# A macaron block of two layers on one core: weights of the first feed-forward pair kept, loads moved to the start, table terms placed one by one

## The chip, the core and the metric

The program runs on one NeuronCore of a Trainium2 chip. Its engines run side by side and meet only at semaphores: TensorE (PE, matrix products into the eight PSUM banks; PEld are its weight loads), VectorE (DVE), ScalarE (ACT), GpSimd (POOL) and SyncE (SP), which here only issues DMAs. Each engine takes its instructions strictly in the order of its program. The metric is the device time of one execution in microseconds (us), the median of several runs; lower is better.

## What is computed

x is 1024 tokens of 256 features. Six sublayers are added to it one after another, each behind a layer norm:

```
x = x + 0.5 * L0_ffn(norm(x))     # f=0, u=0
x = x +       L0_attn(norm(x))    #      u=1
x = x + 0.5 * L0_ffn(norm(x))     # f=1, u=2
x = x + 0.5 * L1_ffn(norm(x))     # f=2, u=3
x = x +       L1_attn(norm(x))    #      u=4, a gated delta rule
x = x + 0.5 * L1_ffn(norm(x))     # f=3, u=5

L0_ffn(x): h = silu(x @ gate_w.T * gate_s) * (x @ up_w.T * up_s);  h @ down_w.T * down_s   # 704 inner features
L1_ffn(x): the same without scales, 688 inner features, each weight = lut[idx], lut of 16 values
L0_attn:   16 heads of 128 over 4 key/value heads, rotary tables, window of 64, difference of two softmaxes, then @ Wo
```

All is float32. The weights of L1_ffn aren't given as numbers but as indices into the table of 16 values; they have to be made on the chip.

## The kernel before

X (tokens in rows) stays in SBUF. Everything else shares one buffer, `arena`, whose columns are laid out anew for each stage: `Arena(arena, start).take(...)` hands out consecutive columns. Two names with the same columns mean that the second may be written only when the first isn't needed any more; the waits see to that.

A feed-forward `ffn(f, u)` works on two halves (hf) of 512 tokens. The 704 or 688 inner features are six tiles (MT), in the order of TILES, the short one first. For each tile PE makes gate and up products (`ffn_up`, lines 631 and 639) into two pairs of banks, ACT takes the SiLU of the gate (`silu`, L998), DVE multiplies with up (`ffn_hidden`, L1344 for f < 2, L1348 else): this is h, and `h_done` counts it. PE may fill a pair of banks again only when the h of the tile two before is done. The down-product (`ffn_down`, L658) of a half wants all six h of it; it is made in two pairs of token tiles, and DVE adds each to X (`ffn_add`, L1359 scales, L1362 adds, and gives `x_ready`). PE's order in a stage: six tiles of half 0; transposes of half 1 of the normed x (`ln_turn`, L614; ACT copies them to XT, L987); two tiles of half 1; down-product of half 0; four tiles of half 1; transposes of half 0 for the next stage; down-product of half 1.

The table's values. While f=0 and f=1 run, ACT and DVE make the L1 weights, half of them in each. For each of the 16 values k, ACT writes `AWAY = |FAR * idx - FAR * k|` (`away`, L1009, 128x2144), zero where idx is k and huge elsewhere; DVE folds `W1 = min(W1, AWAY - value)` (`look_up`, L1382 for k=0 and L1385, two instructions of 1072 columns). One k is called a term here. W1 then holds the negated weights, and SP stores them to DRAM (L561, L588) and loads them from there as f=2's weights. `TERMS` says how many terms stand behind each tile's h: (1, 2, 1, 2, 1, 2) in half 0 and (1, 1, 1, 2, 1, 1) in half 1. ACT has them ahead of the tile's SiLU, DVE behind the tile's h. AWAY has four slots (PENS), and ACT waits for DVE when all are in use. DVE's first sum of half 0 stands behind the second h of half 1.

SP issues the loads in one queue. `load_ffn(f)` loads WU (gate and up), WD (down) and DS (down's scale), in that order, three DMAs, 48 on `w_loaded`; PE and DVE start stage f when 48 * (f + 1) is reached. WU1, the L1 gate and up weights, has the same columns as WU. The attention lays its own tiles over all of these columns, so f=1 loads the f=0 weights again, with the indices' second half into IDX, when the attention's sums are done (`x_ready` 8); f=2's load waits for `x_ready` 12, the end of f=1. The attention's key and value weights WKV lie in OT's last columns at the top of the arena; a_wkv is issued behind `x_ready` 4 and `xt_ready` 8, with the rotary tables, masks and first WQ behind it.

In the attention PE makes keys, values and queries (`rope_project` L686, `values` L693), and then runs a staggered loop over 64 pairs of heads and token tiles (76 steps with the tail). ACT copies the weighted values into OT, 16 heads of 1024 tokens (`ot_copy`, L1063), and `weighted` (L741) multiplies them with WO a group of four heads at a time, 16 steps or more behind; DVE adds to X. The delta rule follows a hand-written table of places (PLACE), which the change doesn't touch.

## Time and profile before

| | us |
|---|---|
| median of 3 runs | 1812.22 |
| lowest, highest | 1808.32, 1816.23 |
| profiled execution | 1804.4 |
| its span, first to last instruction | 1802.4 |

The profile is of one execution. Its times count from the first instruction. A row of a timeline stands for one or more instructions of one engine and line that follow each other; the number in brackets is how long the engine stood idle before them, and the name behind the arrow is what ended the wait. Matmuls are recorded twice for each product of float32, so x8 are the four matmuls that the program has. Their ends are modelled.

The stages lie so in this execution: f=0 from 15 to 93, attention from 100 to 412, f=1 from 421 to 503, f=2 from 512 to 580, the delta rule from 584 to 1721, f=3 from 1729 to 1797.

### The profile page before, as it was taken

What the parts mean: (1) busy time and instruction counts of PE and PEld (TensorE: products, weight loads), DVE (VectorE), ACT (ScalarE), POOL (GpSimd) and SP (SyncE); (2) the same over time, 40 slices, a digit from 0 to 9 for tenths busy, and PEclk for the clock granted to TensorE, in tenths of its full rate; (3) what the DMA queues carried; (4) which work ended last, traced back from release to release, by engine and by line L of the source; (5) the groups of instructions that cost most, each with busy time, mean ns of one, the idle gap of its engine ahead of it and who ended that gap; (6) DMA issues with size and microseconds to landing.
All of it is one profiled execution on the core that took longest, in us unless ns stands there. A gap on an engine that the chain in (4) does not pass through costs nothing. (4 is left out here: it accounts for less than half of the span.)

```text
span 1802.4 us, 33031 instructions
## 1 busy us (share of the span) xinstructions
PE 1547.0 (86%) x10840; PEld 1067.9 (59%) x10840; DVE 1338.2 (74%) x3718; ACT 1034.1 (57%) x2716; POOL 41.3 (2%) x49
## 2 busy tenths in 40 slices
PE   6867889786878778999999998999999899888678
PEld 2534555563535246767766766776777677677535
DVE  6649989956722388889889889888898998984121
ACT  6317878876310455866766676586676667643210
POOL 0000000000000000000000000000000000000000
PEclk9989899989889879999999999999999999989589
DMA  2023000001010211011201101111110110100010
GB/s 103 25 75 93 11 10 5 2 1 77 25 52 18 63 29 43 16 52 51 61 12 55 58 12 57 58 38 29 57 55 12 60 54 16 45 28 7 1 52 24
DMA packets 84071, 69.42 MB, mean 39 GB/s; under 512 B 58673, under 2 KB 72625, under 8 KB 82625
## 3 DMA queue, kind: packets, MB, share of 16 engines
q1 hardware_dynamic: 83904, 67.31, 12.3%
q8 instruction: 91, 1.49, 0.3%
q14 instruction: 76, 0.61, 0.1%
HBM read 58.33 MB, written 6.98 MB: 36 GB/s over the span
## 5 line engine op out<-in xcount | busy, mean ns | idle before, releaser
L1524 DVE SCALAR_TENSOR_TENSOR arena<-arena 128x1024 f32<-128x1024 f32 x144 | 184.1, 1279 | 30.6 <-ACT arena L1101 29.8
L789 PE MATMUL bank<-xt,arena 128*128 128x512 f32 x384 | 197.4, 648 | 4.5 <-ACT arena L1093 3.1
L1582 DVE COPY_PREDICATED arena<-arena,bank 128x512 f32<-128x512 int32 x160 | 185.0, 1175 | 0.3 <-issue 0.3
L842 PE MATMUL bank<-arena 128*64 128x64 f32 x3072 | 143.8, 238 | 36.6 <-DVE arena L1604 21.7
L842 PEld LDWEIGHTS bank<-arena 128*64 128x64 f32 x3072 | 117.0, 144 | 84.0 <-issue 54.6
L1602 DVE TENSOR_TENSOR arena<-arena 128x512 f32<-128x512 f32 x224 | 156.4, 698 | 3.3 <-PE bank L842 2.9
L639 PE MATMUL bank<-xt,arena 128*128 128x512 f32 x320 | 143.5, 604 | 5.5 <-DVE arena L1344 3.9
L789 PEld LDWEIGHTS bank<-xt,arena 128*128 128x128 f32 x384 | 73.7, 209 | 74.8 <-issue 71.8
L639 PEld LDWEIGHTS bank<-xt,arena 128*128 128x128 f32 x320 | 60.3, 193 | 89.6 <-issue 83.6
L658 PE MATMUL bank<-arena 128*128 128x256 f32 (+2 forms) x384 | 102.3, 416 | 11.0 <-DVE arena L1344 10.2
L1100 ACT COPY arena<-bank 128x512 f32<-128x512 f32 x96 | 56.5, 589 | 91.7 <-PE bank L789 91.7
L1035 ACT ACTIVATE arena<-arena 128x128 f32<-128x128 f32 x256 | 99.1, 389 | 6.6 <-DVE arena L1452 6.6
L886 PE MATMUL bank<-arena 128*128 128x64 f32 x512 | 98.4, 273 | 0.0
L658 PEld LDWEIGHTS bank<-arena 128*128 128x128 f32 (+2 forms) x384 | 72.2, 200 | 42.1 <-issue 21.4
L884 PE MATMUL bank<-arena 128*128 128x64 f32 x512 | 95.5, 267 | 0.9 <-DVE arena L1624 0.5
L1211 ACT COPY arena<-bank 128x128 f32<-128x128 f32 x128 | 34.3, 268 | 104.8 <-PE bank L917 104.4
L1604 DVE TENSOR_TENSOR arena<-arena 128x256 f32<-128x256 f32 x224 | 94.1, 420 | 0.0
L686 PE MATMUL bank<-xt,arena 128*128 128x512 f32 x160 | 83.8, 652 | 10.0 <-DMA arena<-a_wkv 5.6
L1220 ACT COPY arena<-bank 128x128 f32<-128x128 f32 x128 | 34.1, 266 | 93.6 <-PE bank L925 57.4
L884 PEld LDWEIGHTS bank<-arena 128*128 128x128 f32 x512 | 79.1, 191 | 9.5 <-DVE arena L1624 6.2
L905 PEld LDWEIGHTS bank<-arena 128*128 128x128 f32 x224 | 40.5, 199 | 71.3 <-issue 42.9
L998 ACT ACTIVATE arena<-bank 128x512 f32<-128x512 f32 (+1 forms) x24 | 14.3, 596 | 117.8 <-PE bank L639 75.4
(169 smaller groups left out, 3563.6 us busy)
## 6 DMA issues: line engine op xcount, KB each, us to landing
arena<-zero_scratch SPq DMA_DIRECT2D x29, 512.0 KB, 3.8
arena<-d_w SPq DMA_DIRECT2D x16, 519.0 KB, 6.1
arena<-beta_scratch SPq DMA_DIRECT2D x16, 512.0 KB, 5.4
arena<-f_up SPq DMA_DIRECT2D x2, 1408.0 KB, 6.3
arena<-w_scratch SPq DMA_DIRECT2D x2, 1376.0 KB, 6.1
arena<-f_idx SPq DMA_DIRECT2D x2, 1072.0 KB, 9.7
w_scratch<-arena SPq DMA_DIRECT2D x2, 1072.0 KB, 4.0
arena<-a_wq SPq DMA_DIRECT2D x16, 128.0 KB, 2.7
```

The lines of the kernel that those rows point to most:

```text
L639: last = pe.matmul(bank[2 * w + n % 2][0:rows, :], (WU if f < 2 else WU1R)[:, w, k, m * P:m * P + rows], XT[:, k, hf * HALF:(hf + 1) * HAL ...
L658: last = pe.matmul(bank[4 + pair][:, j * D:(j + 1) * D], HT[0:rows, hf, m, t * P:(t + 1) * P], WD[0:rows, m, :], start=(m == 0), stop=(m = ...
L686: last = pe.matmul(bank[6 + m % 2][:], w, XT[:, k, hf * HALF:(hf + 1) * HALF], start=(k == 0), stop=(k == KC - 1))
L789: last = pe.matmul(bank[b][:], DW[:, par, c:c + P], XT[:, k, rhs], start=(k == 0), stop=(k == KC - 1))
L842: last = pe.matmul(to[:, :, p], KL[:, par, r], rhs, start=True, stop=True)
L884: pe.matmul(to[:, 0], YY[:, par, c, :], PM[:, c, :].rearrange("p (b r s) -> p b r s", r=2, s=s)[:, :, 0, :], start=True, stop=True)
L886: last = pe.matmul(to[:, 1], PM[:, c, :], YY[:, par, c, :].rearrange("p (b r s) -> p b r s", r=2, s=s)[:, :, 1, :], start=True, stop=True)
L1035: last = act.activation(EX[:, p % 2, i, a, :], SMK[:, p % 2, i, a, :], ACT.Exp, bias=NMX[:, p % 2, i, a:a + 1], scale=-1.0, accum_out=ES[: ...
L1524: dve.scalar_tensor_tensor(out=CT[:, x], in0=RAW[:, x, 3 - j:3 - j + S], scalar=DW[:, par, tap:tap + 1], in1=CT[:, x], op0=ALU.mult, op1=A ...
L1582: dve.copy_predicated(out, mask, bank[b][:].rearrange("p (c b s) -> p c b s", c=8, s=s)).then_inc(free[b], 1)
L1602: dve.tensor_tensor(kq, kq, left, ALU.mult)
L1604: dve.tensor_tensor(kl, kl, t[:, :, 1, :].broadcast_to([P, nb // 2, s]), ALU.mult).then_inc(kq_step, 1)
```

## The change

- Arena: WU, WD, DS and WKV get columns of their own at the top, beside the attention's tiles. So does IDX1, the second half of the indices. To make room OT has 8 heads' slots rather than 16, used in turn; ACT's copy into a slot waits (`wo_done`) for the product of the group two before. WU1 and WD1, the L1 weights, lie in the lower columns, apart from WU and WD.
- SP: a_wkv and the second half of f1_idx are issued at the start, behind f=0's loads. Nothing is loaded for f=1. The load for f=2 goes out when the stored weights have landed in DRAM (`w1_saved`), with no wait for `x_ready` 12. f=2 and f=3 load two tiles, without DS. The counts that PE and DVE wait for are W_COUNT = 48, 48, 80, 112.
- The terms: one behind each of the six tiles of half 0; in half 1 none behind the first h, two behind the second, then the first sum, two more, the second sum and the statistics, one behind these and one behind each of the next three h, and two behind the last. ACT's order follows it: its SiLU stands ahead of its Abs in half 1's first two tiles.

The diff, cut to its core:

```diff
-TERMS = ((1, 2, 1, 2, 1, 2), (1, 1, 1, 2, 1, 1))
+W_COUNT = 48, 48, 80, 112
+TERMS = (1, 1, 1, 1, 1, 1, 2, 2, 1, 1, 1, 1, 2)
...
-        WU = A.take(2, KC, F0)
-        WD = A.take(MT, D)
-        WU1 = arena[:, NT * D:NT * D + 2 * KC * F1]
+        WU1 = A.take(2 * KC * F1)
...
-        DS = A.take(D)
+        WD1 = A.take(MT, D)
...
-        top = arena.shape[1] - H * S
-        OT = arena[:, top:].rearrange("p (h s) -> p h s", h=H)
-        WKV = arena[:, top + (H - 2) * S:].rearrange("p (k n) -> p k n", k=KC)
+        top = arena.shape[1] - (8 * S + KC * 2 * G * P + 2 * KC * F0 + MT * D + D + LW)
+        A = Arena(arena, top)
+        OT = A.take(8, S)
+        WKV = A.take(KC, 2 * G * P)
+        WU = A.take(2, KC, F0)
+        WD = A.take(MT, D)
+        DS = A.take(D)
+        IDX1 = A.take(LW, dt=I32)
...
             def load_ffn(f):
-                up, down = (f0_up, f0_down) if f < 2 else (w1_dram[:, 0:UP1], w1_dram[:, UP1:])
-                sp.dma_start(WU1 if f >= 2 else WU, up).then_inc(w_loaded, 16)
-                sp.dma_start(WD, down).then_inc(w_loaded, 16)
+                if f:
+                    sp.dma_start(WU1, w1_dram[:, 0:UP1]).then_inc(w_loaded, 16)
+                    sp.dma_start(WD1, w1_dram[:, UP1:]).then_inc(w_loaded, 16)
+                    return
+                sp.dma_start(WU, f0_up).then_inc(w_loaded, 16)
+                sp.dma_start(WD, f0_down).then_inc(w_loaded, 16)
                 sp.dma_start(DS, f0_ds).then_inc(w_loaded, 16)
...
             sp.dma_start(IDX, f1_idx[:, 0:LW]).then_inc(idx_loaded, 16)
+            if count > 1:
+                sp.dma_start(WKV, a_wkv).then_inc(at_kv_w, 16)
+            if count > 2:
+                sp.dma_start(IDX1, f1_idx[:, LW:]).then_inc(idx_next, 16)
...
                 sp.wait_ge(xt_ready, 8)
-                sp.dma_start(WKV, a_wkv).then_inc(at_kv_w, 16)
...
                 sp.wait_ge(x_ready, 8)
-                load_ffn(1)
-                sp.dma_start(IDX, f1_idx[:, LW:]).then_inc(idx_loaded, 16)
                 sp.wait_ge(lut_acc, 4 * LUTN)
                 sp.dma_start(w1_dram[:, LW:], W1).then_inc(w1_saved, 16)
                 sp.wait_ge(w1_saved, 32)
             if count > 3:
-                sp.wait_ge(x_ready, 12)
                 load_ffn(2)
...
                 def ot_copy(p):
                     k, t = divmod(p, NT)
                     act.wait_ge(pv_done, p + 1)
-                    act.copy(OT[:, 2 * k:2 * k + 2, t * P:(t + 1) * P],
+                    wait(act, wo_done, 4 * (k // 2 - 2) + t // 2 + 1 if k > 3 else 0)
+                    act.copy(OT[:, 2 * k % 8:2 * k % 8 + 2, t * P:(t + 1) * P],
...
             def ffn(f, u):                      # ACT
+                for q in range(MT):
+                    away(f, terms(q))
+                    silu(f, 0, [q])
                 ln_copy(u, 1)
+                silu(f, 1, [0])
+                away(f, terms(MT))
+                silu(f, 1, [1])
+                away(f, terms(MT + 1))
+                for q in range(2, MT):
+                    away(f, terms(MT + q))
+                    silu(f, 1, [q])
+                away(f, terms(2 * MT))
...
```

Three places in the order of the instructions. First DVE in f=0, from the first h of half 1 (it reads small_vectors_high) to the terms behind the statistics (L1344 is an h and L1385 the terms, two rows of instructions each; L1359 and L1362 scale and add, and L1312 to L1317 are the statistics). Before:

```order
L1344 SCALAR_TENSOR_TENSOR arena<-bank,small_vectors_high,arena 64x512
L1385 SCALAR_TENSOR_TENSOR arena<-arena,small_vectors 128x1072 x2
L1344 SCALAR_TENSOR_TENSOR arena<-bank,small_vectors,arena 128x512
L1359 TENSOR_TENSOR arena<-bank,arena 128x512
L1362 SCALAR_TENSOR_TENSOR x<-arena,x 128x512
L1359 TENSOR_TENSOR arena<-bank,arena 128x512
L1362 SCALAR_TENSOR_TENSOR x<-arena,x 128x512
L1312 BN_STATS ln_stats<-x 128x6 x4
L1315 BN_AGGR ln_mean_var<-ln_stats 128x2 x4
L1317 TENSOR_SCALAR ln_var_eps<-ln_mean_var 128x4
L1385 SCALAR_TENSOR_TENSOR arena<-arena,small_vectors 128x1072 x2
```

And now (L1357 the h, L1398 the terms, L1372 and L1375 the sum):

```order
L1357 SCALAR_TENSOR_TENSOR arena<-bank,small_vectors_high,arena 64x512
L1357 SCALAR_TENSOR_TENSOR arena<-bank,small_vectors,arena 128x512
L1398 SCALAR_TENSOR_TENSOR arena<-arena,small_vectors 128x1072 x4
L1372 TENSOR_TENSOR arena<-bank,arena 128x512
L1375 SCALAR_TENSOR_TENSOR x<-arena,x 128x512
L1398 SCALAR_TENSOR_TENSOR arena<-arena,small_vectors 128x1072 x4
L1372 TENSOR_TENSOR arena<-bank,arena 128x512
L1375 SCALAR_TENSOR_TENSOR x<-arena,x 128x512
L1325 BN_STATS ln_stats<-x 128x6 x4
L1328 BN_AGGR ln_mean_var<-ln_stats 128x2 x4
L1330 TENSOR_SCALAR ln_var_eps<-ln_mean_var 128x4
L1398 SCALAR_TENSOR_TENSOR arena<-arena,small_vectors 128x1072 x2
```

Four terms now stand between the second h and the second sum; behind the statistics four stand ahead of the last h, where five stood.

Second SP, from the first indices to the attention's tables, before:

```order
L559 DMA arena<-f1_idx 128x2144
L561 DMA w1_scratch<-arena 128x2144 [waits lut_acc]
L568 DMA arena<-a_wkv 128x2048 [waits xt_ready,x_ready,w1_saved]
L571 DMA arena<-rope_in 128x1024 x2
L571 DMA arena<-mask_in 64x2x128 x2
L573 DMA arena<-a_wq 128x256 x4
```

and now:

```order
L566 DMA arena<-f1_idx 128x2144
L568 DMA arena<-a_wkv 128x2048
L570 DMA arena<-f1_idx 128x2144
L572 DMA w1_scratch<-arena 128x2144 [waits lut_acc]
L581 DMA arena<-rope_in 128x1024 [waits xt_ready,x_ready,w1_saved]
L581 DMA arena<-rope_in 128x1024
L581 DMA arena<-mask_in 64x2x128 x2
L583 DMA arena<-a_wq 128x256 x4
```

a_wkv and the second indices have moved up past the first save, with no wait of their own.

Third SP again, from the attention's last WQ to the loads for the delta rule, before:

```order
L582 DMA arena<-a_wq 128x256 [waits rope_proj] x12
L465 DMA arena<-f0_up 128x2816 [waits x_ready]
L466 DMA arena<-f0_down 128x1536
L467 DMA arena<-f0_ds 128x256
L586 DMA arena<-f1_idx 128x2144
L588 DMA w1_scratch<-arena 128x2144 [waits lut_acc]
L465 DMA arena<-w1_scratch 128x2752 [waits x_ready,w1_saved]
L466 DMA arena<-w1_scratch 128x1536
L467 DMA arena<-f0_ds 128x256
L471 DMA arena<-d_fa 128x512 [waits x_ready]
```

and now:

```order
L592 DMA arena<-a_wq 128x256 [waits rope_proj] x12
L596 DMA w1_scratch<-arena 128x2144 [waits lut_acc,x_ready]
L469 DMA arena<-w1_scratch 128x2752 [waits w1_saved]
L470 DMA arena<-w1_scratch 128x1536
L478 DMA arena<-d_fa 128x512 [waits x_ready]
```

Five loads are gone, and the load of the new weights waits for the save alone.

## Rows read from the trace of the kernel before

**Rows 1.** The page, part 1: busy us (share of the span) and instructions.
```profile
PE 1547.0 (86%) x10840; PEld 1067.9 (59%) x10840; DVE 1338.2 (74%) x3718; ACT 1034.1 (57%) x2716; POOL 41.3 (2%) x49
```

**Rows 2.** Timeline of PE, f=0 and the attention's door: start, us, engine, line.
```profile
30.66 7.11 PE L639 MATMUL bank<-xt,arena 128*128 128x512 f32 x16 [0.28 <-DVE arena L1344]
37.60 1.04 PE L614 MATMUL bank<-ident,arena 128*128 128x128 f32 x8
...
77.86 14.22 PE L658 MATMUL bank<-arena 128*128 128x256 f32 x48 [5.05 <-DVE arena L1344]
...
105.55 5.79 PE L686 MATMUL bank<-xt,arena 128*128 128x512 f32 x8 [5.57 <-DMA arena<-a_wkv]
```

**Rows 3.** Timeline of DVE in f=0, from the second sum on.
```profile
58.04 0.69 DVE L1359 TENSOR_TENSOR arena<-bank,arena 128x512 f32<-128x512 f32 x1 [4.54 <-PE bank L658]
...
61.33 2.58 DVE L1385 SCALAR_TENSOR_TENSOR arena<-arena,small_vectors 128x1072 f32<-128x1072 f32 x2
63.83 0.74 DVE L1344 SCALAR_TENSOR_TENSOR arena<-bank,small_vectors,arena 128x512 f32<-128x512 f32 x1
64.49 2.57 DVE L1385 SCALAR_TENSOR_TENSOR arena<-arena,small_vectors 128x1072 f32<-128x1072 f32 x2
```

**Rows 4.** Timelines of PE and ACT in f=2, where the halves meet.
```profile
533.35 1.04 PE L614 MATMUL bank<-ident,arena 128*128 128x128 f32 x8
535.11 1.92 PE L631 MATMUL bank<-xt,arena 128*48 128x512 f32 x8 [0.72 <-ACT xt L987]
...
537.06 0.59 ACT L998 ACTIVATE arena<-bank 48x512 f32<-48x512 f32 x1 [2.01 <-PE bank L631]
```

**Rows 5.** Timeline of PE in f=1 and at the start of f=2.
```profile
420.87 3.38 PE L631 MATMUL bank<-xt,arena 128*64 128x512 f32 x8 [1.98 <-DMA arena<-f_ds]
...
445.75 1.04 PE L614 MATMUL bank<-ident,arena 128*128 128x128 f32 x8
...
486.08 16.55 PE L658 MATMUL bank<-arena 128*128 128x256 f32 x48 [5.12 <-DVE arena L1344]
512.52 3.62 PE L631 MATMUL bank<-xt,arena 128*48 128x512 f32 x8 [9.90 <-DMA arena<-f_ds]
```

**Rows 6.** Timeline of ACT in f=1; waits from 412 to 515 (us, times, longest).
```profile
423.41 2.08 ACT L1009 ACTIVATE arena<-arena,minus_far_times_k 128x2144 f32<-128x2144 int32 x1 [3.90 <-DMA arena<-f_idx]
...
PE bank L639 <- DVE arena L1344: 3.6, 3, 2.0
```

**Rows 7.** Windows: us, busy (instructions) of PE, PEld, DVE, ACT, POOL; granted clock; DMA.
```profile
77.90:81.90 4.00, 4.00 (x10) 3.16 (x10) 2.39 (x2) 0.00 (x0) 0.00 (x0) 0.50 0.23 96
...
132.00:134.80 2.80, 0.00 (x0) 0.00 (x0) 2.74 (x4) 0.15 (x1) 0.00 (x0) 1.00 0.78 182
134.90:138.00 3.10, 3.10 (x22) 1.62 (x23) 1.46 (x11) 1.65 (x8) 0.00 (x0) 1.00 1.11 212
```

**Rows 8.** Timelines of SP's issues and of DVE at the attention's first rope.
```profile
100.71 0.33 SPq L568 DMA_DIRECT2D arena<-a_wkv  x1
...
488.54 0.33 SPq L588 DMA_DIRECT2D w_scratch<-arena  x1
504.15 0.33 SPq L465 DMA_DIRECT2D arena<-w_scratch  x1
...
109.44 0.69 DVE L1431 TENSOR_TENSOR arena<-bank,arena 128x512 f32<-128x512 f32 x1 [7.91 <-PE bank L686]
```

**Rows 9.** DMA issues from 485 to 515 and from 0 to 30: KB, us to landing.
```profile
w_scratch<-arena SPq DMA_DIRECT2D x1, 1072.0 KB, 4.0
arena<-w_scratch SPq DMA_DIRECT2D x1, 768.0 KB, 7.2
arena<-f_ds SPq DMA_DIRECT2D x1, 128.0 KB, 7.5
...
arena<-f_idx SPq DMA_DIRECT2D x1, 1072.0 KB, 10.0
```

**Rows 10.** Timeline of PE at the start of f=3.
```profile
1729.22 3.65 PE L631 MATMUL bank<-xt,arena 128*48 128x512 f32 x8 [2.03 <-DMA arena<-f_ds]
```

56 lines of the change are left out of this document (26 added, 30 removed).

## The prediction

> **What bounds the kernel now.** I read the page first: PE is busy for 86% of the span and DVE for 74%, but these are averages over stages with different limits [rows 1]. The change touches only the two feed-forwards of the first pair (f=0 and f=1), the start of f=2 and f=3, and the start of the attention; so next I looked, in PE's timeline, for each stretch in which PE stands still there and for what releases it. In f=0 PE stands 0.28 us for a product of DVE in the first half, 5.05 us before the last down-product, which then runs 14.22 us, and 5.57 us at the attention's door for the DMA of a_wkv [rows 2]. In f=1 it waits three times, 3.6 us in all, for DVE's h in the first half, 1.98 us for f_ds at the start, and 5.12 us before the last down-product, which takes 16.55 us; then f=2 begins after another 9.90 us behind f_ds [rows 5, 6]. That is where time can be had. DVE's timeline says why PE waits for it: after the sums of the first half (58.04) it works without a break until the last h [rows 3].
>
> **The table's terms (TERMS).** A term (two instructions of 1072 columns) is 2.50 us of DVE (61.33 to 63.83), an h 0.66 (63.83 to 64.49; 0.74 until it is out), the sum and statistics 3.29 (58.04 to 61.33) [rows 3]. From the second sum to PE's last down-product is 77.86 - 58.04 = 19.82 us [rows 2, 3], and it holds five terms before and four after, as the order in the section on the change shows: 17.32 us. What matters is when this chain can start. Let L be the start of the transposes that end the first half's up-products. With one term a tile DVE needs 3.16 us a tile, and PE 7.11/2, about 3.5 us [rows 2], so PE no longer waits there. From f=2, where PE is not held up, the first up tile of the second half starts at L + 1.76 and its SiLU at L + 3.71 [rows 4]. ACT's order in the change is SiLU (0.7), two Abs (2.08 each [rows 6]), SiLU; DVE's second h is therefore ready at about L + 9.95, later than PE's tile would allow. Then two terms (L + 14.95), the first sum (1.44, L + 16.4), two terms: L + 21.4. The first half's down-product starts at L + 7.2 and, even at the slow 14.22 us [rows 2], is over by L + 21.4, so it is DVE that holds this stretch. The last down-product starts at L + 21.4 + 17.3 = L + 38.7. PE stands still in two smaller places: about 2 us before the fifth tile of the second half, which wants the third h (L + 21.4 + 3.29 + 2.50 + 0.74 = L + 27.9; PE is there at L + 26), and, two tiles and the transposes later, about 2.8 us before the last down-product.
>
> For f=0, L is 37.60 - 0.28 = 37.32, and the down-product starts at 76.0 in place of 77.86: **1.85 us**. Its length is the first unknown. After the 5.05 us of standing still PE ran at the 1.2 GHz level (granted 0.50) for the first 4 us, and the down-product took 14.22 us. Where PE stood still for 2.9 us at 132, the granted clock stayed 1.00 behind the gap [rows 7]; the same 48 matmuls at 2.4 GHz take 11.9 us. Bounds: 0 to 2.35 us. I take **2.35**, because a gap of 2.8 us is nearer to the one at 132 than to one of 5; the lower end stays in the range. The two terms after the last h (5 us) lie beside this down-product and the first pair's sum waits for PE longer than that, so they cost nothing; were the down-product under 10 us, they would hold up the sums.
>
> **The attention's door.** a_wkv was issued at 100.71, 0.1 us after the last XT was copied [rows 8]; PE's first projection waited for its landing until 105.55 [rows 2]. With WKV loaded at the start PE waits for the copy alone and goes on at about 100.65. What is late next? The cosines and masks, which DVE needs: they are still issued behind XT, with one issue and 1024 KB less ahead of them. They had landed at the latest at 109.44, when DVE began and PE was its last wait [rows 8]; left there, DVE would be done reading the first product at 111.5 (three of its four instructions of 0.69), and PE wants that reading for its third projection, 9.1 us behind its first (5.8 for two projections, 3.4 for two tiles of values), at 109.8. With the megabyte gone they come some 2.4 us earlier (its 4.8 us from issue to landing, 105.55 - 100.71, of which I take half for its bytes), and PE does not wait. PE's whole shift counts: **4.9 us**. The lower bound is 3.2, the constants staying where they are.
>
> **f=1 and the door to f=2.** Weights and indices are there already. PE starts with the XT copy, which ended where ACT's wait began (423.41 - 3.90 = 419.5 [rows 6]), in place of 420.87 [rows 5]: 1.3 us. ACT had to wait 3.90 us for the indices [rows 6]; this and the pairs of terms made PE's 3.6 us of waits [rows 6], which go. So L = 445.75 - 1.3 - 3.6 = 440.8 [rows 5], and the last down-product starts at 440.8 + 38.7 = 479.5 (486.08 before). The terms end two terms behind the last h: before, the save was issued 2.46 us after the down-product's start (488.54 [rows 8]); now one term more, 4.95: at 484.45. Then it is a chain of DMAs: the save lands after 4.0 us, the load of the upper part goes out 0.1 later and that of the down part 0.4 after it, and this lands after 7.2 [rows 9]: 496.1. Before, this load waited for x_ready at 504.15 [rows 8] because it overwrote the weights in use, and f_ds came as a third. PE would be done with f=1 at 491.4 at 2.4 GHz and at 496.1 if it crawls for 16.55 us as before: in both cases the weights are last, and the clock after the gap is worth nothing here. f=2 starts at 496.1 in place of 512.52: **16.4 us**, with the 1.3 in it. Bounds: 11 (no gain from spreading) to 17.5. The save has an x_ready wait ahead of it on SP, long met.
>
> **The rest.** f=3: without f_ds (issued 0.5 us behind the down part, landing 7.5 us later [rows 9]) PE starts about 0.9 us before 1729.22 [rows 10]: **0.9**, at most 2.03. OT with eight slots: ACT's copy gets a wait on wo_done of the group two before. That product is queued on PE 14 to 19 steps of the loop ahead of the copy that waits; it costs nothing unless PE falls so far behind. The delta rule keeps its order and its addresses: nothing.
>
> **Early loads.** a_wkv and the second half of the indices (2.1 MB) are now issued right behind f1_idx, whose landing (10.0 us after its issue [rows 9]) is just when ACT wants it. The landings of the six loads followed their order of issue, so I price this at 0; bound: were f1_idx to share with both, up to 7 us later, of which PE would feel 3 to 5. The Trainium skill, DMA: Bandwidth & Descriptors, section Queues, rings and completion order, says that each DMA engine takes the descriptors of one queue in ring order, but that completion is not first in, first out. By its first half the delay is nothing and the sum stays; by its second, the landing could slip, which is the third rival below.
>
> **The sum.** 1.85 + 2.35 + 4.9 + 16.4 + 0.9 = 26.4 us. Against the profiled execution (span 1802.4, 1804.4 us with what lies around it) that gives 1778.0. That execution lies 7.8 us under the median of 1812.22, and the three runs span 8 us; the same 26.4 off the median is **1785.8 us**.
>
> **The rivals.**
> 1. The clock falls in f=0 after all. For it: DVE leaves PE two gaps within 12 us. Against it: the gap at 132. The sum is 24.1 without the 2.35: 1788.
> 2. Spreading the terms does nothing, because ACT's two Abs ahead of the second SiLU hold DVE as long as the term saved. In f=0 nothing is won (-4.2), and f=2 starts about 5 us later than forecast: 16.9 in all, 1795. For it: the order of ACT. Against it: DVE still has one term fewer in the last stretch, which no wait can put back.
> 3. Early loads delay the first indices: 3 us at the start, so 1789.
> 4. More than forecast: PE, standing still more briefly at the doors, gets its full clock back sooner in the first projections (8 matmuls took 5.79 us [rows 2], at 2.4 GHz they are 3.8) and before f=2. Some 3 us: 1783.
> 5. Slower than before: ACT's new wait in the attention. There are 32 such copies; the wait turns the scale when each holds ACT for 26.4/32 = 0.83 us, that is if the output product on PE came more than 14 steps late, and with 1.0 us each the kernel would be at 1818. From a_wkv's door to f=1 (105.55 to 420.87) lie about 76 steps, 4 us each [rows 2, 5], so PE would have to be 50 us behind. I see no row for that.
> 6. The change does not do what it says at f=2: if the save had to wait for something else behind x_ready, the 11 us of overlap would be gone: 15 in all, 1797. The order of SP shows only w1_saved before the load.
>
> **How the numbers follow.** Forecast 0.55, rival 1 0.13, rival 2 0.10, rival 3 0.07, rival 4 0.09, rival 5 0.01, rival 6 0.02, something unseen 0.03. The forecast alone is good to 4 us either way for the spread of the runs. The range from 1777 to 1797 takes in rivals 1 to 4 with a little of that spread. A measurement of this kernel can tell about 0.5% from no change, that is 9 us (1803.2). All cases but 5 and the unseen are below: faster 0.95, same 0.04, slower 0.01.
>
> **What would show it.** In the changed profile: PE's L639 tiles of the first halves without a wait for DVE; a wait of about 2 us before the fifth tile and about 2.8 before the last down-product in both f=0 and f=1, and that product of f=0 at 11.9 us; the first projection directly behind the XT copy, with DVE's first rope about 1.5 us behind PE's first product; f=1's first Abs directly behind its XT copy; the load of w1 issued 4.1 us after the save, and PE at f=2 still waiting for a DMA, at about 487.0 (25.5 us ahead of 512.52). I am wrong if PE waits for wo or the cosines in the attention, if f=0's start slips, or if the delta rule's span, which should be the same, moves by more than 3 us.

## The result and the profile after

The change took the kernel from 1811.65 us (median of 6 runs, 1805.46 to 1816.23) to **1786.05 us** (median of 6, 1782.94 to 1791.28). The two medians are 25.6 us apart; the ratio of the runs is 0.9869 (23.7 us), with a 95% interval of 0.9848 to 0.9891, so 19.7 to 27.5 us less. The forecast was 1785.8, from 26.4 us of gain. The total agrees; the terms below it agree less well, and the experiments show by how much.

The profiled execution of after took 1788.14 us, its span is 1786.4. First the page, part 1, against [rows 1]: the busy times are nearly those of before (PE has 5 us more), the span is shorter.

```profile
PE 1552.1 (87%) x10840; PEld 1073.6 (60%) x10840; DVE 1338.7 (75%) x3718; ACT 1034.0 (58%) x2716; POOL 41.3 (2%) x49
```

PE's timeline of after from f=0 to the attention's door answers to [rows 2]. L665 is the down-product, L638 and L646 the up tiles, L621 the transposes, L693 and L700 the attention's projections and values:

```profile
14.97 3.36 PE L638 MATMUL bank<-xt,arena 128*64 128x512 f32 x8 [1.74 <-ACT xt L994]
18.27 17.43 PE L646 MATMUL bank<-xt,arena 128*128 128x512 f32 x40
35.54 1.04 PE L621 MATMUL bank<-ident,arena 128*128 128x128 f32 x8
...
63.74 7.10 PE L646 MATMUL bank<-xt,arena 128*128 128x512 f32 x16 [2.08 <-DVE arena L1357]
70.68 1.04 PE L621 MATMUL bank<-ident,arena 128*128 128x128 f32 x8
74.39 12.00 PE L665 MATMUL bank<-arena 128*128 128x256 f32 x48 [2.67 <-DVE arena L1357]
92.32 1.97 PE L621 MATMUL bank<-ident,arena 128*128 128x128 f32 x8 [5.93 <-DVE arena L1339]
95.05 6.03 PE L693 MATMUL bank<-xt,arena 128*128 128x512 f32 x8 [0.77 <-ACT xt L994]
```

The 40 matmul records of the first half run with no wait for DVE. Two waits of 2.08 and 2.67 us are left, and the down-product takes 12.00 us where it took 14.22. The first projection waits for the XT copy alone.

The same engine in f=1 and at the start of f=2, against [rows 5]:

```profile
409.63 3.68 PE L638 MATMUL bank<-xt,arena 128*64 128x512 f32 x8 [0.72 <-issue]
413.24 17.71 PE L646 MATMUL bank<-xt,arena 128*128 128x512 f32 x40
...
469.32 12.00 PE L665 MATMUL bank<-arena 128*128 128x256 f32 x48 [2.67 <-DVE arena L1357]
486.33 3.66 PE L638 MATMUL bank<-xt,arena 128*48 128x512 f32 x8 [5.02 <-DMA arena<-w_scratch]
489.92 18.62 PE L646 MATMUL bank<-xt,arena 128*128 128x512 f32 x40
```

f=2 starts at 486.33, 26.2 us earlier than at 512.52, and still behind a DMA. SP's issues there, against [rows 8], are the save and, 4 us behind it, the two loads:

```profile
474.32 0.33 SPq L596 DMA_DIRECT2D w_scratch<-arena  x1
478.34 0.33 SPq L469 DMA_DIRECT2D arena<-w_scratch  x1
478.71 0.43 SPq L470 DMA_DIRECT2D arena<-w_scratch  x1
```

For the comparisons below I cut each profile into stages at PE's rows: A from f=0's first up-product to its last down-product's start, B from there to the attention's first projection (B holds that product), C the attention up to the transposes ahead of f=1, D from these to f=2's first up-product, E from there to the delta rule's first product, F from there to f=3's first up-product, G the rest. All in us. A median in brackets is the one profiled execution, where no others were timed; each ratio is against runs of before taken beside it, so it isn't quite the median divided by 1811.65.

| kernel | A | B | of B, the product | C | D | E | F | G | median | ratio to before |
|---|---|---|---|---|---|---|---|---|---|---|
| before | 62.85 | 27.69 | 14.22 | 311.39 | 95.58 | 74.58 | 1142.12 | 73.18 | 1811.65 | 1 |
| before, again | 62.88 | 29.76 | 14.68 | 312.87 | 92.63 | 74.70 | 1149.04 | 73.18 | (1812.39) | |
| after | 59.42 | 20.66 | 12.00 | 311.90 | 79.38 | 75.80 | 1151.82 | 72.45 | 1786.05 | 0.9869 |
| after, again | 59.36 | 23.95 | 15.28 | 315.37 | 79.34 | 75.81 | 1146.53 | 73.39 | (1790.58) | |
| after, third | 59.58 | 20.66 | 12.00 | 312.04 | 79.54 | 75.72 | 1146.07 | 73.51 | 1786.17 | 0.9868 |
| terms alone | 60.33 | 27.19 | 12.00 | 315.81 | 85.80 | 74.70 | 1148.18 | 72.00 | 1801.74 | 0.9940 |
| loads alone | 62.79 | 23.29 | 14.62 | 315.80 | 80.31 | 73.33 | 1148.78 | 73.32 | 1795.23 | 0.9906 |
| load waits | 60.15 | 20.67 | 12.00 | 316.08 | 83.80 | 75.32 | 1151.67 | 72.31 | 1793.49 | 0.9910 |
| tight | 54.39 | 20.67 | 12.00 | 313.25 | 77.43 | 75.11 | 1145.60 | 73.48 | 1774.42 | 0.9809 |
| in place | 60.61 | 25.32 | 16.65 | 311.86 | 74.31 | 74.38 | 1149.24 | 71.90 | 1783.17 | 0.9839 |
| both | 55.31 | 20.67 | 12.00 | 310.84 | 69.80 | 74.39 | 1152.82 | 72.33 | 1771.58 | 0.9779 |
| both, again | 54.75 | 20.66 | 12.00 | 312.87 | 70.19 | 74.38 | 1147.09 | 71.96 | 1772.02 | 0.9785 |
| later loads | 59.97 | 20.66 | 12.00 | 315.89 | 79.35 | 74.20 | 1146.76 | 72.35 | (1786.10) | |

In the two first profiles A, B and D gain 3.43, 7.03 and 16.20 us and E loses 1.22: 25.4 in all. But F, in which no instruction of the delta rule was changed, is 9.7 us longer in after. My prediction had named just that as a sign of being wrong, so this was the first thing to settle.

### The profile page after: what moved, and what is told of

It reads as the page before. It is cut to its first block and busy times, and to the rows that moved or that the text cites. A ratio compares the mean times of both kernels' runs of the same rounds, so it can differ in the third digit from the quotient of the medians.

```text
span 1786.4 us, 33061 instructions
## 1 busy us (share of the span) xinstructions
PE 1552.1 (87%) x10840; PEld 1073.6 (60%) x10840; DVE 1338.7 (75%) x3718; ACT 1034.0 (58%) x2716; POOL 41.3 (2%) x49
## 3 DMA queue, kind: packets, MB, share of 16 engines
q8 instruction: 91, 1.49, 0.4%
## 5 line engine op out<-in xcount | busy, mean ns | idle before, releaser
L796 PE MATMUL bank<-xt,arena 128*128 128x512 f32 x384 | 204.7, 669 | 4.5 <-ACT arena L1106 3.1
L849 PE MATMUL bank<-arena 128*64 128x64 f32 x3072 | 143.6, 238 | 36.8 <-DVE arena L1619 22.3
L646 PE MATMUL bank<-xt,arena 128*128 128x512 f32 x320 | 142.6, 602 | 3.8 <-DVE arena L1357 3.8
L646 PEld LDWEIGHTS bank<-xt,arena 128*128 128x128 f32 x320 | 60.4, 193 | 86.8 <-issue 86.6
L665 PE MATMUL bank<-arena 128*128 128x256 f32 (+2 forms) x384 | 95.6, 395 | 6.2 <-DVE arena L1357 5.3
L665 PEld LDWEIGHTS bank<-arena 128*128 128x128 f32 (+2 forms) x384 | 67.9, 189 | 34.8 <-issue 20.5
L693 PE MATMUL bank<-xt,arena 128*128 128x512 f32 x160 | 83.1, 648 | 5.3 <-DVE arena L1450 4.5
L891 PEld LDWEIGHTS bank<-arena 128*128 128x128 f32 x512 | 80.4, 194 | 9.7 <-DVE arena L1639 5.9
L912 PEld LDWEIGHTS bank<-arena 128*128 128x128 f32 x224 | 40.8, 199 | 67.1 <-issue 39.4
L893 PEld LDWEIGHTS bank<-arena 128*128 128x128 f32 x512 | 78.8, 194 | 0.0
```

The costliest lines, as they stand in the source:

```text
L646: last = pe.matmul(bank[2 * w + n % 2][0:rows, :], (WU if f < 2 else WU1R)[:, w, k, m * P:m * P + rows], XT[:, k, hf * HALF:(hf + 1) * HAL ...
L665: last = pe.matmul(bank[4 + pair][:, j * D:(j + 1) * D], HT[0:rows, hf, m, t * P:(t + 1) * P], (WD if f < 2 else WD1)[0:rows, m, :], start ...
L693: last = pe.matmul(bank[6 + m % 2][:], w, XT[:, k, hf * HALF:(hf + 1) * HALF], start=(k == 0), stop=(k == KC - 1))
L796: last = pe.matmul(bank[b][:], DW[:, par, c:c + P], XT[:, k, rhs], start=(k == 0), stop=(k == KC - 1))
L849: last = pe.matmul(to[:, :, p], KL[:, par, r], rhs, start=True, stop=True)
L891: pe.matmul(to[:, 0], YY[:, par, c, :], PM[:, c, :].rearrange("p (b r s) -> p b r s", r=2, s=s)[:, :, 0, :], start=True, stop=True)
```

## Experiments

### The delta rule: the change or the chip?

Theory: the 9.7 us are the chip's variation from one execution to the next. Rival: something in the change (addresses of buffers, phase of the DMAs) costs the delta rule 10 us. The edit is none: both kernels were profiled once more.

> The kernel before, profiled once more, unchanged. The question is the delta rule: with the same instructions in both kernels it took 1109.9 us before and 1121.7 us after, from the first matmul of its prelude to its last product. Theory: this is the chip's own variation from run to run (the stretches in which the granted clock is at 1.2 GHz fall elsewhere), so this second profile may give anything between some 1107 and 1125 us. Rival: the change has made the delta rule 12 us longer; then this profile gives 1110 us within 3 us.

> The kernel after, profiled once more, unchanged. Theory (variation of the chip): the delta rule takes anything between some 1107 and 1125 us. Rival (the change's doing): 1122 us within 3 us, and about 12 us more than in the second profile of the kernel before. In both cases feed-forward 0, the attention's door and feed-forward 1 repeat the first profile of after within 0.3 us each: last down-product of feed-forward 0 at about 74.4 us, first key projection at 95.0, first up-product of feed-forward 2 at about 486.3.

(The expectations cut the delta rule a little shorter than stage F does; the difference between the two first profiles is 11.8 us by that cut and 9.7 us by F.)

Windows over F in the two profiles of before (us, then busy us of PE, PEld, DVE, ACT, POOL with their instructions, granted clock, DMA):

```profile
587.10:1729.22 1142.12, 1012.11 (x8128) 757.01 (x8129) 925.87 (x2182) 702.92 (x1578) 28.15 (x18) 0.94 0.14 40
```

```profile
587.98:1737.02 1149.04, 1019.54 (x8129) 761.59 (x8129) 926.56 (x2182) 701.66 (x1578) 28.14 (x18) 0.93 0.14 40
```

and in the first and the third of after:

```profile
562.13:1713.95 1151.82, 1025.57 (x8128) 766.78 (x8129) 925.90 (x2181) 701.77 (x1578) 28.18 (x18) 0.92 0.14 40
```

```profile
562.52:1708.59 1146.07, 1016.34 (x8129) 759.32 (x8129) 925.84 (x2181) 702.17 (x1578) 28.17 (x18) 0.93 0.14 40
```

DVE's, ACT's and POOL's busy times agree within 1.3 us everywhere; PE's busy time for the same 8128 matmul records runs from 1012 to 1026 us, and the granted clock from 0.94 down to 0.92 with it. That is where the difference lies: PE spent more of F at 1.2 GHz. The second profile of before has 6.9 us more than its first, and after came to 1146.5 and 1146.1 the next two times, below that second profile of before. The rival fell: 9.7 us are not the change's. The second expectation had a miss of its own. Its first key projection was due at 95.0 and came at 98.36, because the down-product ahead of it took 15.28 us and not 12.00; with a longer attention on top of that, f=2 started at 493.07 and not at 486.3. Over all thirteen profiles F lies between 1142.1 and 1152.8, the first profile of before being the shortest of all; a cost of the change of 2 or 3 us (mean 1146.4 of the three profiles with the old buffers, 1148.6 of the ten with the new) can't be excluded by so few. The attention C varies in the same way, from 310.8 to 316.1.

Against this, the stages that the change touches repeat closely wherever the clock is the same: D is 79.38, 79.34 and 79.54 in after, and B is 20.66 or 20.67 in all seven profiles that have the new loads and that product at 12.00 us.

### One part at a time

First the new order of the terms with the old buffers and loads, as a diff against the kernel before:

```diff
-TERMS = ((1, 2, 1, 2, 1, 2), (1, 1, 1, 2, 1, 1))
+TERMS = (1, 1, 1, 1, 1, 1, 2, 2, 1, 1, 1, 1, 2)
...
+                silu(f, 1, [0])
+                away(f, terms(MT))
+                silu(f, 1, [1])
+                away(f, terms(MT + 1))
...
+                look_up(f, terms(MT))
+                ffn_add(f, u, 0, [0])
+                look_up(f, terms(MT + 1))
+                ffn_add(f, u, 0, [1])
```

> The kernel before with nothing but the new spread of the table's terms (the pens' order on ScalarE and the order on VectorE); buffers and loads as before. Theory: feed-forward 0 ends 4.2 us earlier (1.85 us of chain and 2.35 us because the down-product stays at 2.4 GHz, 11.9 us and not 14.2), the door of the attention is unchanged (key and value weights still loaded behind the save), and feed-forward 2 starts some 9 us earlier, since the values of the second half end with the last down-product and no longer behind it: about 13 us less than before, ratio 0.993. Rival 2 of the prediction (ScalarE's pens hold VectorE, spreading does nothing): 1811 us, ratio 1.000.

Measured: 1801.74 us, ratio 0.9940 (0.9918 to 0.9962). Rival 2, that ScalarE's absolute values cancel the gain, is out. Stage D went from 95.58 and 92.63 to 85.80, and A from 62.9 to 60.3. At the door a part was given back: the wait for a_wkv was 7.30 us, as it was 7.17 in the second profile of before, and not 5.57 as in the first [rows 2]. PE's rows at the door in the terms-only kernel:

```profile
75.42 12.00 PE L658 MATMUL bank<-arena 128*128 128x256 f32 x48 [2.67 <-DVE arena L1349]
...
102.61 6.69 PE L686 MATMUL bank<-xt,arena 128*128 128x512 f32 x8 [7.30 <-DMA arena<-a_wkv]
```

Then the new buffers and early loads with the old order of the terms:

```diff
-        WU1 = arena[:, NT * D:NT * D + 2 * KC * F1]
+        WU1 = A.take(2 * KC * F1)
...
+            if count > 1:
+                sp.dma_start(WKV, a_wkv).then_inc(at_kv_w, 16)
+            if count > 2:
+                sp.dma_start(IDX1, f1_idx[:, LW:]).then_inc(idx_next, 16)
...
-                load_ffn(1)
-                sp.dma_start(IDX, f1_idx[:, LW:]).then_inc(idx_loaded, 16)
...
-                sp.wait_ge(x_ready, 12)
```

> The kernel before with nothing but the new buffers and early loads (first pair's weights kept beside the attention, key and value weights and second indices loaded before the attention, feed-forward 2's weights loaded behind the save); the table's terms in the old order. Theory: feed-forward 0 as before (last down-product at 77.9 us, 14.2 us long), door 4.9 us shorter, feed-forward 2 starts about 18.5 us earlier than before in all, feed-forward 3 gives 0.9: about 19.4 us less than before, ratio 0.989. The sum of this and of the spread alone (13 us) is above the 26 us of both, since with both in place feed-forward 2 waits for the values' end and the loads behind it. Rival: the loads are all of the gain, 26 us, ratio 0.986.

Measured: 1795.23 us, ratio 0.9906 (0.9873 to 0.9938), 16.4 us under the median of before; by stages B and D together went from 123.3 and 122.4 to 103.6, some 19 us. With the old order the values are done so late in f=1 that PE has only just finished when the loads land:

```profile
482.60 13.68 PE L665 MATMUL bank<-arena 128*128 128x256 f32 x48 [5.12 <-DVE arena L1352]
497.27 1.93 PE L638 MATMUL bank<-xt,arena 128*48 128x512 f32 x8 [0.98 <-DMA arena<-w_scratch]
```

PE's wait is 0.98 us where it is 5.02 in after. So the two parts overlap. It shows in stage D: alone they shorten it by 8.3 and 13.8 us against the mean of before, together by 14.7 and not by 22. The ratios point the same way (0.60% and 0.94% alone, 1.31% for both), but their intervals are too wide to show it by themselves. The rival's ratio (loads are all of it, 0.986) lies outside the interval. In after it is the order of the terms that brings the save forward, and the chain of save and loads that keeps PE from using all of it.

### Where does f=2's start come from?

```diff
             if count > 3:
+                sp.wait_ge(x_ready, 12)
                 load_ffn(2)
```

> The kernel after, but SyncE waits for the whole result of feed-forward 1 before it issues the loads of feed-forward 2, as it did before the change. Theory: these loads (3.7 us of issue and landing ahead of the first up-product) now start when the last output of feed-forward 1 is there and not when the save of the values is issued, so feed-forward 2 starts some 4.4 us later (first up-product at about 490.7 us, not 486.3) and the kernel takes about 1790.5 us. Rival (feed-forward 2's start is set by the values alone): no change, 1786. Rival (the loads come another 7 us late because their landing needs more than the 4 us between save and load): 1797.

Stage D was 83.80 us against 79.42 (the mean of after's three), 4.4 us more, as expected, and PE's wait grew by the same:

```profile
474.37 12.00 PE L666 MATMUL bank<-arena 128*128 128x256 f32 x48 [2.67 <-DVE arena L1358]
495.80 3.65 PE L639 MATMUL bank<-xt,arena 128*48 128x512 f32 x8 [9.43 <-DMA arena<-w_scratch]
```

The median, 1793.49 (ratio 0.9910, 0.9874 to 0.9945), is 7.4 us over after; the interval is 13 us wide and takes in the 4.4. Both rivals fell by the stage, which is the sharper measure.

Now the other way: make the second half of the values where f=2 reads them, so that nothing has to be stored and loaded before f=2. The first half is loaded early in f=1; the save remains for f=3.

```diff
-W_COUNT = 48, 48, 80, 112
+W_COUNT = 48, 48, 64, 96
...
+        W1B = arena[:, NT * D + LW:NT * D + 2 * LW]
...
+                sp.dma_start(WU1[:, 0:LW], w1_dram[:, 0:LW]).then_inc(w_loaded, 16)
                 sp.wait_ge(lut_acc, 4 * LUTN)
-                sp.dma_start(w1_dram[:, LW:], W1).then_inc(w1_saved, 16)
+                sp.dma_start(w1_dram[:, LW:], W1B).then_inc(w1_saved, 16)
                 sp.wait_ge(w1_saved, 32)
-            if count > 3:
-                load_ffn(2)
...
                 pe.wait_ge(w_loaded, W_COUNT[f])
+                if f == 2:
+                    pe.wait_ge(lut_acc, 4 * LUTN)
...
+                    W1K = (W1, W1B)[f]
...
             def delta_rule():
+                dve.wait_ge(w1_saved, 32)
```

> The kernel after, but the second half of feed-forward 2's values is made directly in the columns from which feed-forward 2's matmuls read it; only the first half is loaded, early in feed-forward 1, and the save to DRAM (for feed-forward 3) hides. Theory: TensorE's 5.0 us wait for the loads ahead of feed-forward 2 goes, its first up-product starts at about 481.3 us, and with no gap the clock stays at 2.4 GHz there (first tile 1.9 us and not 3.7): 5 to 8 us less, about 1779. Rival: the values' last term on VectorE is itself as late as the loads (after the last down-product), so that the wait for DMA becomes a wait for VectorE of 3 us and more: 1 to 3 us less.

PE in this kernel goes from f=1's last product into f=2 without a wait, and the clock holds:

```profile
475.25 12.00 PE L665 MATMUL bank<-arena 128*128 128x256 f32 x48 [2.68 <-DVE arena L1359]
487.18 1.92 PE L638 MATMUL bank<-xt,arena 128*48 128x512 f32 x8
```

D and E are 5.1 and 1.4 us shorter than in after, 6.5 together: the theory's 5 to 8. The rival (the last term is too late on VectorE) fell: the values' last four instructions end at 480.2, 7 us ahead of PE.

```profile
475.11 5.07 DVE L1401 SCALAR_TENSOR_TENSOR arena<-arena,small_vectors 128x1072 f32<-128x1072 f32 x4
```

The median, 1783.17 (0.9839, 0.9796 to 0.9881), is only 2.9 us under after. This profile also shows f=0's down-product at 16.65 us, 4.65 us lost to the clock in a stage that the edit doesn't touch; whether the timed runs had as much of that isn't known. The interval, 15 us wide, doesn't tell 2.9 from 6.5.

### Is the order of the terms the best?

In after two terms stand between the first and the second sum, and two between the second h and the first sum. PE stands still twice behind them. This edit moves one term from between the two sums to a place ahead of the second h, and one from ahead of the last h to the very end. ScalarE's order follows: it has one absolute value ahead of the second SiLU of half 1 where after has two, and five ahead of the third:

```diff
-TERMS = (1, 1, 1, 1, 1, 1, 2, 2, 1, 1, 1, 1, 2)
+TERMS = (1, 1, 1, 1, 1, 1, 1, 2, 1, 1, 1, 1, 0, 3)
...
-                away(f, terms(MT))
+                away(f, range(6, 7))
                 silu(f, 1, [1])
...
                 ffn_hidden(f, 1, [0])
-                ffn_hidden(f, 1, [1])
                 look_up(f, terms(MT))
-                ffn_add(f, u, 0, [0])
+                ffn_hidden(f, 1, [1])
                 look_up(f, terms(MT + 1))
+                ffn_add(f, u, 0, [0])
+                look_up(f, terms(MT + 2))
                 ffn_add(f, u, 0, [1])
```

(The expectation's first words are loose: two terms still stand between the second h and the first sum, and one between the sums. And ScalarE has fewer absolute values ahead of the second SiLU, not more.)

> The kernel after with the terms put a little further from the critical chain: the second sum directly behind its two SiLUs (no term of the table ahead of it), two pens' worth of ScalarE's absolute values moved ahead of the second SiLU of the second half, three terms at the very end. Theory: the second sum stands 19.1 us behind the first SiLU's tile and not 21.4, the fifth tile's first half has no stall (2.1 us before), and the last down-product starts 4.6 us earlier in feed-forward 0 and 1; in feed-forward 1 the values end later than the last down-product, so feed-forward 2 starts only about 2 us earlier: about 6.6 us less than after, 1779.5. Rival (ScalarE's absolute values hold VectorE, not VectorE's own order): VectorE gains the same waits on ScalarE that it loses in work, no change, 1786.

First two rows of DVE's timeline of after in f=0, its second h and its second sum:

```profile
45.12 0.75 DVE L1357 SCALAR_TENSOR_TENSOR arena<-bank,small_vectors,arena 128x512 f32<-128x512 f32 x1 [4.33 <-ACT arena L1005]
...
57.08 0.68 DVE L1372 TENSOR_TENSOR arena<-bank,arena 128x512 f32<-128x512 f32 x1
```

Then the tight kernel. The moved term fills a part of the 4.33 us in which DVE waited for ScalarE, so the second h starts as before, at 45.17, and the second sum at 54.65, 2.43 us earlier (2.3 expected).

```profile
42.56 2.58 DVE L1401 SCALAR_TENSOR_TENSOR arena<-arena,small_vectors 128x1072 f32<-128x1072 f32 x2 [1.77 <-ACT arena L1016]
45.17 0.75 DVE L1360 SCALAR_TENSOR_TENSOR arena<-bank,small_vectors,arena 128x512 f32<-128x512 f32 x1
45.84 5.07 DVE L1401 SCALAR_TENSOR_TENSOR arena<-arena,small_vectors 128x1072 f32<-128x1072 f32 x4
50.82 0.69 DVE L1375 TENSOR_TENSOR arena<-bank,arena 128x512 f32<-128x512 f32 x1
...
54.65 0.68 DVE L1375 TENSOR_TENSOR arena<-bank,arena 128x512 f32<-128x512 f32 x1
```

PE has no wait left behind it in f=0; the four tiles of the second half (x32) and the last down-product follow at once:

```profile
54.52 14.00 PE L646 MATMUL bank<-xt,arena 128*128 128x512 f32 x32
68.36 1.04 PE L621 MATMUL bank<-ident,arena 128*128 128x128 f32 x8
69.46 12.00 PE L665 MATMUL bank<-arena 128*128 128x256 f32 x48
```

A fell by 5.1 us to 54.39 and D by 2.0 to 77.43, 7.1 in all where 6.6 were expected; the rival, no change, fell with that. D gives less than A because f=2 waits for the DMAs anyway: 7.57 us now and not 5.02. The median, 1774.42 (0.9809, 0.9769 to 0.9849), is 11.6 us under after, 4.5 more than A and D explain; the interval, 14 us wide, takes this in. In the profile B is 1.1 us shorter than the mean of after's three (one of those three had the slow down-product), E 0.7 and F 2.5; F varies by more than that by itself.

Both edits together, without a diff of their own:

> Both edits together (second sum without a term ahead of it; second half of the values made in place). Theory: 4.6 us in feed-forward 0, 4.6 us in feed-forward 1, which no longer end in the save and load chain, 5 us of feed-forward 2's wait, and up to 3 us of clock: some 17 us less than after, 1769. Rival: with three terms at the very end, VectorE ends the values after the last down-product, and feed-forward 2 waits for it: 10 us less, 1776.

1771.58 us, ratio 0.9779 (0.9749 to 0.9809): 14.5 us under after, where 17 were expected. The 9.6 us of D came (79.42 to 69.80), but of the 3 us allowed for the clock E gave 1.4. Then the same kernel once more with after beside it on one chip, neither changed:

> The kernel after unchanged, timed on the same chip as the next one, and a third profile of it. Whole time about 1787 us. Stage from the first transposes of feed-forward 1 to feed-forward 2's first up-product 79.4 us within 0.1; last down-product of feed-forward 0 either 12.0 us (clock at 2.4 GHz through it) or 15 to 17 us (falls to 1.2 GHz within it), as both have been seen with the 2.7 us wait ahead of it.

> Tighter order and values made in place, once more, beside the kernel after on the same chip. Stage by stage against after: feed-forward 0 is 3.8 to 5.0 us shorter, feed-forward 1 9.6 us (69.8 and not 79.4), feed-forward 2 1.4 us (74.4 and not 75.8), the rest the same: 14.8 to 16 us less than after, about 1771. With no wait ahead of feed-forward 0's last down-product, this takes 12.0 us again. Rival (the gain of the first measurement was mostly luck of the clock in the untouched stages): 8 us less or under.

After came to 1786.17 (0.9868, 0.9839 to 0.9897) and the kernel with both edits to 1772.02 (0.9785, 0.9752 to 0.9818), 14.15 us less, the two intervals apart. By stages A, D and E (means of two and of three profiles) are 4.4, 9.4 and 1.4 us shorter, 15.2 in all. That is more than the 7.1 and 6.5 of the two edits alone, since with the tighter order alone PE waited 7.57 us for the loads, and this wait goes too. PE at f=1's end and f=2's start, from the first profile of both edits:

```profile
459.93 12.00 PE L665 MATMUL bank<-arena 128*128 128x256 f32 x48 [0.17 <-DVE arena L1362]
471.86 1.92 PE L638 MATMUL bank<-xt,arena 128*48 128x512 f32 x8
...
478.68 13.97 PE L646 MATMUL bank<-xt,arena 128*128 128x512 f32 x32 [1.26 <-DVE arena L1366]
```

The new rival (VectorE ends the values too late) shows nowhere: the values end at 467.3, 4.5 us ahead of f=2's first product, which has no wait. The 1.26 us in the last row are another thing: PE wants f=2's first h, and DVE comes to it only when it is done with f=1's sum and the norm, at 477.8. In the first kernel made in place it is 1.27 us. This version beats both kernels: 2.2% under before, 0.8% under after.

### The loads at the start

SyncE holds the two added loads back until the table's first term is done (`lut_acc` counts both instructions of a term, so the expectation's "second term" should read first); they went out at 21.99 and 22.36.

```diff
             sp.dma_start(IDX, f1_idx[:, 0:LW]).then_inc(idx_loaded, 16)
+            sp.wait_ge(lut_acc, 2)
             if count > 1:
                 sp.dma_start(WKV, a_wkv).then_inc(at_kv_w, 16)
```

> The kernel after, but the key and value weights and the second indices are loaded only when the table's second term is done, well after the first indices have landed. Theory (the queue serves its loads in their order, so the two new ones hardly delay what stands ahead of them): the first absolute value on ScalarE starts at once or up to 0.65 us earlier than in after (15.5 us there), nothing else changes, since the first term isn't on the path of feed-forward 0. Rival 3 of the prediction (the early loads hold up the first indices by more): feed-forward 0 becomes shorter than the 59.4 us from first up-product to last down-product by over 1 us.

ScalarE's first absolute value in after, and in this kernel:

```profile
15.48 2.08 ACT L1016 ACTIVATE arena<-arena,minus_far_times_k 128x2144 f32<-128x2144 int32 x1 [0.65 <-DMA arena<-f_idx]
```

```profile
15.03 2.08 ACT L1017 ACTIVATE arena<-arena,minus_far_times_k 128x2144 f32<-128x2144 int32 x1
```

That looks like a wait of 0.65 us taken away, but the second profile of after, with the loads where they were, has none either:

```profile
14.92 2.08 ACT L1016 ACTIVATE arena<-arena,minus_far_times_k 128x2144 f32<-128x2144 int32 x1
```

The landing itself varies. In the four profiles with nothing right behind the indices it took 10.0, 10.1, 10.2 and 10.4 us from their issue; in the nine with 2.1 MB behind them 9.9 to 10.6; the means are 10.2 and 10.1. So the loads cost the indices nothing that these profiles can tell. A is 59.97 us, not below the 59.36 to 59.58 of after. Rival 3 is out.

## Why the prediction was right, point by point

**The chain in f=0** (1.85 us): right in mechanism, too small. From the transposes on it was right to 0.15 us: L + 38.85 where I had L + 38.7 (35.54 to 74.39), with the two waits at 2.08 and 2.67 us for the "about 2" and "about 2.8". What was mis-sized is L, 20.57 us behind the first up-product and not 22.3. I took 0.28 us off for the wait of [rows 2]; but the wait was short only because PE itself was slow ahead of it. The second profile of before shows it:

```profile
18.76 10.57 PE L639 MATMUL bank<-xt,arena 128*128 128x512 f32 x24
30.81 7.11 PE L639 MATMUL bank<-xt,arena 128*128 128x512 f32 x16 [1.49 <-DVE arena L1344]
```

There the 24 records take 10.57 us and the wait is 1.49; in the first they take 11.76 and it is 0.28, and both reach the next tile at 30.7 to 30.8. DVE set that time. With DVE out of the way PE's own pace shows, and over its first records that differs from profile to profile: the first 8 up-records take 3.3 to 3.7 us (1.94 in half 1), the 40 behind them 17.43 to 18.30 in the seven profiles with this order, and L is 20.5 to 21.8 us behind the first up-product. The rows give a granted clock of 1.00 there, so they don't show why. So A is 59.4 to 60.6 us, 2.2 to 3.5 less than the 62.8 to 62.9 with the old order, and the first profile of after, with 59.4, is one of the quick ones.

**The clock at the last down-product** (2.35 us, rival 1 the loss of it): right in the first profile and in the third (12.00 us), wrong in the second (15.28). The step that failed is the lower bound of 0 for this term: 15.28 is longer than the 14.22 and 14.68 of before, so the clock can cost more than is to be gained. More on this below.

**The attention's door** (4.9 us): right. B without its product is 13.47 us in before and 8.66 in after, 4.8 less. What I didn't see is that the old door varied: 13.47, 15.08 and 15.19 us in the three profiles with the old loads, and 8.66 to 8.67 in all ten with the new. So it is worth 4.8 to 6.5. The cosines and masks came later than forecast. They landed some 7.3 us behind the end of the last XT copy, where it was some 8.3 in before: 1 us earlier, and not the 2.4 that I took from the megabyte less. This varies too: in the second profile of after they came 5.7 us behind the start of PE's first product, in the first 7.1. DVE's first rope in after:

```profile
102.19 0.69 DVE L1446 TENSOR_TENSOR arena<-bank,arena 128x512 f32<-128x512 f32 x1 [6.37 <-DMA arena<-mask_in]
```

It is 7.1 us behind the start of PE's first product and waits for mask_in. By the prediction's own working it was due 6.4 us behind that start (109.44 less 2.4, with PE at 100.65); the "1.5 us" in its list of signs doesn't fit this working. PE's third projection starts at 104.35, just as DVE has done three of its four instructions (102.19 to 104.29). So PE didn't wait, but the cover that I counted on was used up to the last tenth.

**f=1 and the door to f=2** (16.4 us): right against the first profile, 16.2, with f=2 at 486.33 where I had 487.0. The parts fit one by one: from the transposes ahead of f=1 to L it is 23.83 us and not 28.81, 5.0 less (4.9 forecast); the down-product starts at L + 38.5 (38.7); the save went out 5.0 us behind its start (474.32 after 469.32) and the load 4.0 behind that, as worked out. Against the second profile of before D gains only 13.3: there the clock gave that down-product 13.68 us and not 16.55, and with the old order f=2's load waited for its end.

**f=3** (0.9): 0.4 against the first profile (2.03 to 1.61), 0.7 against the second (2.33 to 1.61).

**The start of f=2**: a term that the sum took for nothing. E is 1.0 to 1.2 us longer in all three profiles of after. Behind the 9.9 us of standing still in before the 40 records of the first half took 17.43 us, with a granted clock of 1.00 from 516 on:

```profile
512.50:516.00 3.50, 3.48 (x8) 0.66 (x8) 0.00 (x0) 0.00 (x0) 0.00 (x0) 0.50 0.00 0
516.00:520.00 4.00, 4.00 (x11) 1.82 (x10) 0.82 (x2) 1.19 (x2) 0.00 (x0) 1.00 0.00 0
```

Behind 5.0 us in after they take 18.62, and the granted clock was 0.71 in the second window from the start of f=2:

```profile
486.00:490.00 4.00, 3.67 (x9) 0.74 (x9) 1.19 (x4) 0.00 (x0) 0.00 (x0) 0.50 0.00 0
490.00:494.00 4.00, 4.00 (x7) 1.86 (x8) 0.69 (x1) 1.19 (x2) 0.00 (x0) 0.71 0.00 0
```

Rival 4 had a gain of clock here; in after it was a small loss. That isn't fixed either: with the loads at the start moved, f=2 stood still for 4.98 us and E was 74.20. Why the clock came back later in three of these four profiles stays open.

**The waits added** (rival 5): in the attention the ACT copy with the new wait shows 1.9 us in all, once, and for PE's product of its own pair, not for wo_done. The stage C is 313.4 us in the mean of the three profiles with the old buffers and 313.6 in the ten with the new. **Rival 6** fell with the load at 478.34, 4.0 us behind the save.

**The sum.** With means over the profiles of each kernel, A, B, D and E gain 3.4, 7.0, 14.7 and -1.1 us, f=3 0.6: 24.5 us before rounding; the medians say 25.6, the ratio 23.7, with 19.7 to 27.5 in the interval. The forecast's 26.4 came so near partly because the term that was too small (A) and the ones that were a little too large (D by the luck of its first profile, f=3, and E's unseen loss) cancel in part; that is luck, not precision. The condition by which I would have been wrong, F moving by more than 3 us, was badly chosen: F moved by 6.9 us between two profiles of before.

## What to carry over

Compare stages, not whole executions: where the rows before and after a stage are the same work, and PE's clock is the same, its length repeats to 0.2 us, while a stage of 1150 us of dense matmuls varies by 6 or 7 us in one kernel and by 10.7 over all thirteen profiles. A small difference between two single profiles, like the 0.65 us of wait above, may be in neither kernel. A wait in a profile is what is left after everything that was late beside it, so ask how long it would be if the waiting engine were at its best. When an order is tuned, look again at what the next wait is: here the values no longer came last, the store and load of them did, and making them in place was worth about as much (6.5 us) as the next step of the order (7.1).

## What was not expected of the hardware

Whether PE's clock holds behind a wait isn't settled by the wait alone. All 26 last down-products of f=0 and f=1 in the 13 profiles, by the wait for DVE right ahead of them:

| wait ahead (us) | products | of them at 12.00 us | the others |
|---|---|---|---|
| 5.05 to 5.12 | 6 | 0 | 13.68, 13.68, 14.22, 14.62, 14.68, 16.55 |
| 2.67 to 2.68 | 14 | 12 | 15.28, 16.65 |
| 0 to 0.17 | 6 | 6 | |

Both exceptions stand in f=0. In the second profile of after everything ahead of the product is as in the first, and the clock still fell; windows over the first 8 us of the product, first in after and then in its second profile:

```profile
74.39:78.39 4.00, 4.00 (x17) 3.03 (x18) 4.00 (x4) 0.36 (x1) 0.00 (x0) 1.00 0.00 0
78.39:82.39 4.00, 4.00 (x18) 3.01 (x17) 2.30 (x3) 0.00 (x0) 0.00 (x0) 1.00 0.58 240
```

```profile
74.41:78.41 4.00, 4.00 (x12) 2.71 (x12) 4.00 (x4) 0.36 (x1) 0.00 (x0) 0.68 0.00 0
78.41:82.41 4.00, 4.00 (x10) 2.96 (x10) 0.92 (x1) 0.00 (x0) 0.00 (x0) 0.50 0.58 240
```

The rows ahead of both are the same to 0.02 us (63.74 and 63.76, 70.68 and 70.70, 74.39 and 74.41), the granted clock is 1.00 just ahead of both; nothing in the program or in PE's rows ahead tells them apart, and what decides stays open. The Trainium skill, TensorE: Matmul & The Clock Gate, section "What's actually happening", calls the number of slow matmuls at the start of a kernel variable from run to run. The traces agree (the 40 records of f=0's first half take 17.43 to 18.30 us in seven profiles with one order of the terms), and show it behind a wait of 2.7 us in the middle of a stage too. An order that leaves PE a wait of at most 0.17 us, as the tight one does, had 12.00 us in all six cases.

The second is how much a single DMA's landing varies, and how little 2.1 MB queued behind it did. With them behind, the first indices landed 9.9 to 10.6 us after their issue in nine profiles, without them 10.0 to 10.4 in four. The Trainium skill, DMA: Bandwidth & Descriptors, section "Queues, rings and completion order", says that each engine takes a ring's descriptors in order, but that completions may pass each other. The first half agrees with these landings, and if the second half had a price here it is hidden in their spread.
